# Two-layer audio tower on one core: the written-out order of all five engines replaced by another one

## What is computed

```python
h = tok(x)                                  # 512 -> 256, bias, layernorm, gamma, beta
h = h + attn0(layernorm(h))                 # 16 heads of 64, softcap 50, causal, sigmoid gates, w_out
h = h + tanh(layernorm(h) @ W @ A1 @ A2 + b)
h = h + attn1(layernorm(h))                 # 16 heads of 16, fenwick mask, projection
h = h + fp4_down(silu(fp4_gate(y)) * fp4_up(y))   # y = layernorm(h); width 704
```

## Time and profile before

| | us |
|---|---|
| median of 3 runs | 356.13 |
| lowest, highest | 355.34, 357.83 |
| the profiled execution, its own time | 355.12 |
| its span, first to last instruction | 353.2 |
| mean granted TensorE clock | 0.947 |

### The profile page before, as it was taken

One profiled execution on the slowest core, in us unless ns is written; L12 is line 12 of the kernel. 1 busy time (PEld: TensorE's weight loads), 2 busy tenths in 40 slices (PEclk: granted clock), 3 DMA queues, 4 the chain that ended last, 5 costly groups with the idle time before them and its releaser, 6 DMA issues.

```text
span 353.2 us, 11732 instructions
## 1 busy us (share of the span) xinstructions
PE 309.1 (88%) x5122; PEld 272.3 (77%) x5122; DVE 242.4 (69%) x527; ACT 115.7 (33%) x259; POOL 28.6 (8%) x49
## 2 busy tenths in 40 slices
PE   4589995999996799999998999997889997699585
PEld 3479975999885589998987899886778876578563
DVE  5789975967582454887645887343568888369992
ACT  3743452442432142334241234433213334012121
POOL 1020400000130000100101101000012100110000
PEclk9969996999996889999999999999999999679899
DMA  7992012000100000000000000000000000000001
GB/s 250 369 357 96 0 52 75 2 2 0 61 2 4 5 2 2 2 3 4 17 3 18 4 2 2 0 17 5 5 2 2 15 3 6 2 2 15 0 2 45
DMA packets 8774, 12.80 MB, mean 36 GB/s; under 512 B 779, under 2 KB 5651, under 8 KB 8725
## 3 DMA queue, kind: packets, MB, share of 16 engines
q1 hardware_dynamic: 8724, 12.06, 10.1%
HBM read 11.01 MB, written 1.05 MB: 34 GB/s over the span
## 4 chain that ended last, share of the span: by engine, by line
PE 77%; DVE 11%; issue 8%; DMA 2%; ACT 1%; SPq 0%; ACTq 0%; DVEq 0%
PE psum L1181 69%; PE psum L1359 2%; DMA wqkv_raw<-in_L_attn_w_qkv_dram 2%; PE psum L1381 2%; PE psum L1484 1%; PE psum L1241 1%; DVE qs L802 1%; PE psum L1461 1%; DVE wqkv_lo L820 1%; DVE xT_lo L820 1%; DVE ln_st L869 1%; DVE hhb L805 1%; DVE hhb L812 0%; DVE wq_s L802 0%; DVE hhb L814 0%
## 5 line engine op out<-in xcount | busy, mean ns | idle before, releaser
L538 POOL TENSOR_TENSOR ln_rs<-ln_mv,minus_half 128x1 f32<-128x1 f32 x40 | 27.4, 690 | 287.5 <-DVE ln_mv L872 287.4
L1181 PE MATMUL psum<-aT_hi,wqkv_hi 128*128 128x256 f32 x128 | 37.6, 294 | 0.4 <-DVE aT_lo L820 0.3
L1181 PE MATMUL psum<-aT_lo,wqkv_hi 128*128 128x256 f32 x128 | 36.1, 282 | 0.0
L1181 PE MATMUL psum<-aT_hi,wqkv_lo 128*128 128x256 f32 x128 | 35.9, 280 | 0.0
L553 ACT ACTIVATE qkT<-psum 128x512 f32<-128x512 f32 x32 | 18.9, 598 | 35.0 <-PE psum L1181 35.0
L1181 PE MATMUL psum<-wout_s,oT 128*128 128x256 f32 x128 | 29.3, 382 | 0.0
L1181 PEld LDWEIGHTS psum<-wout_s,oT 128*128 128x128 f32 x128 | 23.8, 190 | 3.3 <-issue 0.2
L1181 PEld LDWEIGHTS psum<-aT_hi,wqkv_hi 128*128 128x128 f32 x128 | 24.1, 188 | 1.7 <-DVE aT_lo L820 0.5
L1181 PE MATMUL psum<-v_aug,probs 32*32 32x65 f32 x1024 | 21.0, 238 | 3.8 <-issue 3.7
L1181 PEld LDWEIGHTS psum<-aT_lo,wqkv_hi 128*128 128x128 f32 x128 | 24.1, 188 | 0.1
L1181 PEld LDWEIGHTS psum<-aT_hi,wqkv_lo 128*128 128x128 f32 x128 | 24.1, 188 | 0.0
(11 more groups left out here) (222 smaller groups left out, 754.2 us busy)
## 6 DMA issues: line engine op xcount, KB each, us to landing
x_in<-in_x_dram SPq DMA_DIRECT2D x4, 512.0 KB, 5.2
wqkv_raw<-in_L_attn_w_qkv_dram SPq DMA_DIRECT2D x4, 512.0 KB, 6.5
wout_s<-in_L_attn_w_out_dram SPq DMA_DIRECT2D x1, 1024.0 KB, 6.9
out_dram<-res SPq DMA_DIRECT2D x8, 128.0 KB, 1.7
wqkv_raw<-in_L_attn_w_qkv_dram SPq DMA_DIRECT2D x1, 768.0 KB, 7.4
w_raw<-in_L_attn_W_qkv_dram SPq DMA_DIRECT2D x1, 768.0 KB, 9.3
wdn_raw<-in_L_ffn_w_down_dram SPq DMA_DIRECT2D x1, 704.0 KB, 8.1
wgu_raw<-in_L_ffn_w_gate_dram SPq DMA_DIRECT2D x1, 640.0 KB, 6.6
```

The source lines that it names most:

```text
L538: nc.gpsimd.tensor_tensor(ln_rs[:, s, k, j:j + 1], ln_mv[:, s, k, j, 1:2], minus_half[:, :], ALU.pow).then_inc(rstd_ready[f"{k}_{j}"], 1)
L1181: return nc.tensor.matmul(o_, a, b, start=first, stop=last)
```

## The change

Only the table `ORDER` is another one. Stages, their instructions and their waits for inputs are the same; the lists of TensorE, ScalarE, VectorE and GpSimd are permuted throughout, and on SyncE two stores of the last pass change places. The table is one line longer, so every line number behind it is higher by one. Two fewer pure waits stand in TensorE's program. Two lines of the diff show its kind:

```diff
-        qk1_0.3 u1_0.2 bT_1.3 qk1_1.2 sc1_0.3 qk1_1.3 sc1_1.2 val1_0.3 sc1_1.3 val1_1.2 mx1_0.3 mx1_1.2
+        mx1_1.2 sc1_0.3 yT_0.2 o1T_1.2 val1_0.3 bT_1.3 proj_1.2 qk1_1.3 val1_1.3 mx1_0.3 sc1_1.3 o1T_0.3
```

More of the change, by code:

```diff
@@ L45 @@
     "pe": """
[L46 to L60, removed]
@@ L61 @@
-        qk1_0.3 u1_0.2 bT_1.3 qk1_1.2 sc1_0.3 qk1_1.3 sc1_1.2 val1_0.3 sc1_1.3 val1_1.2 mx1_0.3 mx1_1.2
-        o1T_0.3 proj_0.3 val1_1.3 o1T_1.2 mx1_1.3 proj_1.2 o1T_1.3 hT0_0.2 hT1_0.2 proj_1.3 down_0.2 yT_0.3
-        g0_0.3 g1_0.3 u1_0.3 yT_1.2 u0_0.3 g0_1.2 g1_1.2 u0_1.2 u1_1.2 yT_1.3 g0_1.3 g1_1.3 u1_1.3 hT0_0.3
-        u0_1.3 hT1_0.3 hT0_1.2 hT1_1.2 down_0.3 down_1.2 hT0_1.3 hT1_1.3 down_1.3""",
-    "act": """
[L66 to L81, removed]
@@ L82 @@
-    "dve": """
[L83 to L112, removed]
-        he_0.3 hb_1.2 yT_1.3 hc_1.2 hf_0.3 hd_1.2 hg_0.3 he_1.2 sa0_1.3 hf_1.2 hh_0.3 sa1_1.3 hg_1.2 sb1_1.3
-        hh_1.2 sb0_1.3 ha_1.3 hb_1.3 hc_1.3 hd_1.3 he_1.3 hf_1.3 hg_1.3 hh_1.3 down_0.3 down_1.2 down_1.3""",
@@ new lines @@
+        turn_tok xT0.0 bcast tok0.0 xT1.0 tok1.0 xT0.1 turn_ff tok0.1 xT1.1 join_ff1 aT.0 tok1.1 v11.0 v00.0
+        v12.0 qk5.0 qk7.0 qk0.0 v10.0 qk6.0 qk1.0 qk2.0 qk3.0 v01.0 v02.0 qk4.0 aT.1 xT0.2 turn_gate0 s0.0
+        join_ff2 s1.0 turn_gate1 qk3.1 qk2.1 mix0.0 qk4.1 qk0.1 oT01.0 mix1.0 v11.1 oT00.0 qk5.1 qk6.1 qk1.1
+        v02.1 v00.1 qk7.1 turn_up0 v12.1 out0.0 oT10.0 turn_up1 s0.1 v10.1 turn_down s1.1 v01.1 oT11.0 nT_0.0
+        mix0.1 ffn_0.0 out1.0 tok0.2 bT_0.0 mix1.1 oT01.1 qk1_0.0 val1_0.0 oT00.1 nT_1.0 xT1.2 sc1_0.0 ffn_1.0
@@ new lines @@
+        out0.1 mx1_0.0 tok1.2 o1T_0.0 oT10.1 bT_1.0 proj_0.0 oT11.1 xT0.3 qk1_1.0 out1.1 aT.2 val1_1.0 sc1_1.0
+        qk0.2 v10.2 v11.2 v01.2 mx1_1.0 qk5.2 o1T_1.0 qk6.2 proj_1.0 yT_0.0 qk1.2 g0_0.0 g1_0.0 u1_0.0 qk3.2
+        qk2.2 u0_0.0 nT_0.1 v02.2 v00.2 yT_1.0 qk7.2 qk4.2 g0_1.0 s0.2 u0_1.0 g1_1.0 hT0_0.0 u1_1.0 hT1_0.0
+        nT_1.1 s1.2 down_0.0 ffn_0.1 tok0.3 xT1.3 hT0_1.0 hT1_1.0 mix0.2 down_1.0 bT_0.1 ffn_1.1 qk1_0.1
+        tok1.3 bT_1.1 sc1_0.1 v12.2 val1_0.1 val1_1.1 mix1.2 oT01.2 aT.3 qk1_1.1 mx1_0.1 v10.3 o1T_0.1 qk0.3
@@ new lines @@
+        proj_0.1 sc1_1.1 qk7.3 qk2.3 oT00.2 mx1_1.1 v02.3 qk3.3 o1T_1.1 qk5.3 proj_1.1 yT_0.1 qk4.3 g0_0.1
+        v00.3 v12.3 g1_0.1 u1_0.1 u0_0.1 out0.2 qk6.3 v11.3 yT_1.1 qk1.3 g0_1.1 s0.3 g1_1.1 oT11.2 oT10.2
+        u0_1.1 u1_1.1 hT0_0.1 out1.2 nT_0.2 hT1_0.1 v01.3 down_0.1 s1.3 nT_1.2 hT0_1.1 hT1_1.1 ffn_0.2 mix0.3
+        down_1.1 bT_0.2 ffn_1.2 mix1.3 qk1_0.2 oT01.3 oT00.3 val1_0.2 bT_1.2 sc1_0.2 out0.3 mx1_0.2 qk1_1.2
+        o1T_0.2 nT_0.3 oT11.3 oT10.3 ffn_0.3 proj_0.2 sc1_1.2 out1.3 bT_0.3 val1_1.2 qk1_0.3 nT_1.3 ffn_1.3
@@ L115 @@
     "pool": """
[L116 to L119 removed]
+        tok0.0 tokln0.0 tok1.0 tokln1.0 tok0.1 tok1.1 tokln1.1 tokln0.1 ln2_0.0 ln3_0.0 ln2_1.0 tok0.2 ln3_1.0
+        tokln0.2 tok1.2 tokln1.2 ln4_0.0 ln4_1.0 ln2_1.1 ln2_0.1 ln3_0.1 tok0.3 ln3_1.1 tok1.3 tokln1.3
@@ L120 @@
+        tokln0.3 ln4_0.1 ln4_1.1 ln2_0.2 ln2_1.2 ln3_0.2 ln3_1.2 ln2_0.3 ln4_0.2 ones.3 ln3_0.3 ln2_1.3
+        ln3_1.3 ln4_1.2 ln4_0.3 ln4_1.3""",
     "sp": """
-        load.2 wout load.3 store_0.0 store_1.0 store_0.1 store_1.1 store_0.2 store_0.3 store_1.2 store_1.3""",
+        load.2 wout load.3 store_0.0 store_1.0 store_0.1 store_1.1 store_0.2 store_1.2 store_0.3 store_1.3""",
 }.items()}
```

56 lines of the change are left out of this document (52 added, 4 removed).

## The result

| | before | after |
|---|---|---|
| median of 4 runs each | 355.74 us | 336.17 us |
| lowest and highest | 354.21, 357.83 | 333.21, 337.39 |
| ratio, 95% interval | 1 | 0.9434 (0.9355 to 0.9513) |
| profiled execution | 355.12 us | 336.39 us |
| its span, mean granted clock | 353.2 us, 0.947 | 334.5 us, 0.98 |

The forecast was 344 us, 3.4% faster; measured is 5.7%. The time lies at the lower end of the range of 336 to 353, and not safely inside it: the ratio of 0.9434 on the 356.13 us from which the forecast counts gives 335.97. The direction was right, and so were the fetch waits as a cause and most of their places. The gain was forecast too small, above all in its clock term, and nearly half of it needs a look at how the order lies against the pieces.

A forecast was written before the change was run, and what follows sets the result against it. The bound was TensorE, with 22.4 us of issue waits read as instruction fetches. 355.1 - 13.1 (fetches) - 3 (clock) + 3 (new waits) + 1 (tail) = 343.0, plus 1.0 from profiled execution to median: 344 us, range 336 to 353.

The forecast's parts named there:

- clock term: TensorE's five half-clock stretches behind the head: some go with the fetch waits, giving back 3 us, bounds 0 and 8.
- The reading of the bound: TensorE's program comes in pieces of 256 instructions; it stands 22.4 us on issue when the next piece is late.
- Rival 2: TensorE's issue waits are no fetches, or spacing does not hide them; time stays at 356 us; chance 0.06.
- The fetch term: TensorE's instruction-fetch waits fall from 22.4 to 9.3 us, so 13.1 us go, bounds 8 and 15.3.
- the nine pieces summed: TensorE pieces after the change with work shorter than the 3.75 us fetch price, together short by 10.8 us.
- the 2.5 that I asked for: Sign: TensorE's 4.01 us wait at 53 us, where `wout` moves, should shrink below 2.5 us.
- New waits and the tail: TensorE waits that fetches hid: 3 us, bounds 0 and 8; behind the last `mx1_`: 1 us, bounds -1 and 4.
- Rival 1: VectorE takes back what the fetches give; no wait behind 236 us gives anything: 350 us; chance 0.13.
- Rival 3: Slower: layer two's chain comes later on VectorE and TensorE has no cover, 15.9 us in three passes: 360 us; chance 0.05.

The follow-up runs named there:

- bare pieces: Kernel before with 512 small products (2048 instructions, 8 pieces) added at the end of TensorE's order: 382.76 us, ratio 1.0839.
- the three holes: Kernel after, TensorE waiting for one small transfer behind `qk1.2`, two there, or one behind `s0.2`: 337.68, 340.51 and 336.72 us.
- `wout` moved away: Kernel before with the 1 MB load of `wout` issued only when `mix0.0` is done: 353.31 us, ratio 0.9945.
- the version with 2.8 us of issue left: Kernel after with `s1.2` two places later and `mx1_1.2` and `mx1_1.3` two places earlier in TensorE's order: 337.61 us, ratio 0.9553.
- 160 instructions ahead: Kernel after with 40 small products in TensorE's head: 344.86 us, ratio 0.9671; 9.7 us of issue waits where the refitted fetch rule said 19.3.

## Why the prediction was right in the fetches and failed in the clock

**The reading of the bound** held: issue waits of any size at 256th instructions, moved by instructions put ahead, and bare pieces of 3.45 to 4.00 us with a packet for each. Rival 2 (no fetches, 356 us) is out.

**The fetch term** was 13.1 us with bounds of 8 and 15.3; measured 14.9. Of the 10.8 us summed for the order after, 7.5 came, 0.70, where I took the 0.86 of before. The waits stand at five of the nine pieces summed and at `mix0.0`, where the sum had none. `s1.2` was right to 0.05 us; `sc1_0.3` (1.86 forecast, 1.17) and `mx1_1.3` (1.94, 0.58) were too long. The bare price is lower than 3.75 us. `s1.0` shrank to 0.50, below the 2.5 that I asked for.

**The clock term** is the step that failed: "I take 3 us, bounds 0 and 8". TensorE's busy time fell by 8.4 us, just outside the bounds; 6.2 of it is clock loss (11.8 to 5.6), the rest I can't assign. Of the 6.6 us by which the sum fell short in the profile (12.1 against 18.7), 5.4 are this term, 1.8 the fetch term, and the others were 0.6 the other way. I reasoned that where waits remain, stretches of half clock remain, in three neighbouring pieces (`s1.1`, `mix0.1` and the stage behind) and two near the end. Of these five waits three came, 1.72 us at 96, 1.17 and 0.58, and none has half clock behind it. Of the five stretches at fetch waits before, one remains, at `s1.2`, whose 2.27 us are the only fetch wait over 2 us left of four. The two other stretches that remain stand at waits for VectorE, as did the sixth one before, which the prediction left out. So a remaining wait was taken for a remaining stretch whatever its length. That short waits mostly leave the clock alone rests on the three holes, on `wout` moved away and on the count; for a single wait it isn't settled, as `bT_lo_b` shows. Two of the stretches that went had lain on `mix`, small products that took twice as long there.

**New waits and the tail** were 3 and 1 us; measured 4.6 together, and the tail itself 0.0. The 3 us were a guess that no row carried, and that they came so near is luck. Rival 1 (VectorE takes it back, 350 us) didn't come in this kernel. It is what stands next, though: the version with 2.8 us of issue left shows it.

**Rival 3** (slower, 360 us) was not seen, but the two kernels with TensorE's order changed alone ran into what it is made of, TensorE waiting for results that VectorE and ScalarE have not yet: 355.92 and 362.10 us. In the change, the other engines' orders moved with TensorE's.

**What the prediction didn't have at all** is that a sum over boundaries belongs to one lie of the order. It laid the boundaries at their right places, so the fetch term for this kernel was sound; but it called the gain one of spacing. Somewhat under half of it is the lie, by the ratios above. That 344 us, the forecast, is about what this order gives in the mean over its places is a coincidence. Nor did it have that the spacing serves VectorE: with three stages put back, 8.6 us of waits for `k1sa` came and 1.3 us of fetch waits. What stays open is the exact split, why 160 instructions ahead cost only half of the refit, 2.2 us of busy time, and what besides its length decides whether a wait takes the clock.

## What to carry to other kernels

Count instructions, not only time: where TensorE stands on issue at a whole multiple of one number of instructions, runs of tiny products use a piece up before the next is there, and large work between them hides it. An "issue" wait that stands at no such multiple can be something else, as the 2.69 us at `mx1_0.0` were: look at what the stage waits for in its code, and when that was done. Time a change of order at two or three shifts of its start before crediting the order, for here 28 tiny products in an idle head moved the same order by 15 us. And a space between two dependent small stages serves two masters, the fetch and the engine that computes in between; here it was mostly the second, so moving one engine's stages alone cost more than the fetches gave.

## What the runs showed that I had not expected

An order of the same work with the same 41 instruction packets goes from 0.9434 to 0.9861 of the kernel before by nothing but 112 instructions put into its idle head. TensorE's clock stayed at 2.4 GHz behind a hole of 1.20 us and fell to 1.2 GHz behind one of 2.40 at the same place, for 3.4 us, in one execution each. And fetches have a floor even when nothing else moves: 3.45 us for a piece whose products need 1.93 at half clock, with a wait of 1.53 us in each.
